# Layer 0's second product: one 512-column product for h's high part, and a bank emptied in two operations

## What is computed

```python
for i in range(e):                          # 8 experts, top 2 of them for each token
    h = jax.nn.silu(xf @ w1[i] + b1[i])     # 256 -> 1024
    y = h @ w2[i] + b2[i]                   # 1024 -> 256: the "second product"
    out = out + y * comb[:, i:i + 1]
```

## Time and profile before

| | |
|---|---|
| runs shown | 557.59, 560.01 and 751.81 us, median 560.01 |
| profiled execution | 557.76 us |
| its span, first to last instruction | 556.0 us |
| PE busy | 526.5 us, 95% |
| DVE busy | 329.5 us, 59% |
| POOL busy | 248.5 us, 45% |
| granted TensorE clock, mean | 0.995 of 2.4 GHz |

### The profile page before, as it was taken

How to read it: one execution, slowest core, us unless ns; L and a number is a source line. 1 busy time by engine, 2 the same in 40 slices (tenths; PEclk the granted TensorE clock), 3 DMA queues, 4 the chain that set the end, 5 groups by cost and what they waited for, 6 DMA issues and landing times.

```text
span 556.0 us, 15295 instructions
## 1 busy us (share of the span) xinstructions
PE 526.5 (95%) x3516; PEld 467.9 (84%) x3517; DVE 329.5 (59%) x770; ACT 339.9 (61%) x657; POOL 248.5 (45%) x278
## 2 busy tenths in 40 slices
PE   7999979999999999999999999799999999999995
PEld 3887638889999899999878876499999999999894
DVE  5647873555533555555575478745766666767542
ACT  5786625666655666666647856255677676767450
POOL 5659022343644355554354270224545364545432
PEclk9999999999999999999999999899999999999999
DMA  7645745876432454224550428463374656321211
GB/s 256 199 135 151 257 132 164 267 177 164 113 77 39 147 111 96 36 44 124 163 170 7 152 79 284 148 214 93 64 201 111 176 129 161 82 38 29 40 24 20
DMA packets 49037, 70.54 MB, mean 127 GB/s; under 512 B 9182, under 2 KB 40560, under 8 KB 49008
## 3 DMA queue, kind: packets, MB, share of 16 engines
q1 hardware_dynamic: 35216, 56.41, 32.3%
q0 software_dynamic: 10464, 13.58, 13.6%
q10 hardware_dynamic: 3328, 0.20, 0.4%
HBM read 57.55 MB, written 13.47 MB: 128 GB/s over the span
## 4 chain that ended last, share of the span: by engine, by line
PE 75%; DMA 6%; issue 5%; DVE 5%; ACT 3%; DVEq 3%; ACTq 1%; POOL 1%; POOLq 0%; SPq 0%
PE banks L1351 15%; PE banks L1353 15%; PE banks L1352 15%; PE banks L1576 5%; PE banks L1413 5%; PE banks L1501 4%; PE banks L1359 3%; PE banks L1477 3%; DMA expert_io<-xn_dram,gcol 2%; PE banks L1541 2%; PE banks L1631 2%; DMA mid_dram<-region_b,scol 1%; DVEq L1229 1%; PE banks L1424 1%; DMA xres<-in_x_dram 1%
## 5 line engine op out<-in xcount | busy, mean ns | idle before, releaser
L1351 PE MATMUL banks<-w_hi,xT_hi 128*128 x336 | 119.3, 355 | 4.3 <-DVE xT_lo L1220 2.6
L1353 PE MATMUL banks<-w_hi,xT_lo 128*128 x336 | 114.9, 342 | 0.0
L1352 PE MATMUL banks<-w_lo,xT_hi 128*128 x336 | 114.2, 340 | 0.0
L1351 PE MATMUL banks<-w_hi,hT_hi 128*128 x364 | 107.9, 296 | 3.7 <-DVE hT_lo L1298 2.7
L1353 PE MATMUL banks<-w_hi,hT_lo 128*128 x364 | 102.8, 283 | 0.0
L1352 PE MATMUL banks<-w_lo,hT_hi 128*128 x364 | 102.8, 282 | 0.0
L842 ACT COPY banks<-seed_rows 128x672 f32 (+1 forms) x84 | 69.0, 822 | 25.8 <-DVE h_sb L1315 10.3
L652 POOL DMA_INDIRECT mid_dram<-region_b,scol x26 | 49.6, 1909 | 77.3 <-DMA mid_dram<-region_b,scol 28.7
L625 POOL TENSOR_TENSOR w_lo<-raw,w_hi 128x1024 fp32r<-128x1024 f32 (+2 forms) x24 | 58.8, 2467 | 46.3 <-ACT w_hi L697 39.3
L652 POOL DMA_INDIRECT out_dram<-region_b,scol x26 | 46.1, 1772 | 72.2 <-DMA expert_io<-xn_dram,gcol 22.0
L1351 PEld LDWEIGHTS banks<-w_hi,hT_hi 128*128 128x128 f32 x364 | 69.3, 190 | 6.9 <-issue 6.0
(11 more groups left out here) (211 smaller groups left out, 872.0 us busy)
## 6 DMA issues: line engine op xcount, KB each, us to landing
raw<-in_L_ffn_w_dram SPq DMA_DIRECT2D x32, 512.0 KB, 3.8
raw<-in_L_ffn_W_dram SPq DMA_DIRECT2D x16, 672.0 KB, 3.9
seed_rows<-in_L_ffn_b_dram SPq DMA_DIRECT2D x8, 672.0 KB
seed_rows<-in_L_ffn_b_dram SPq DMA_DIRECT2D x8, 512.0 KB
xn_dram<-raw SPq DMA_DIRECT2D x6, 512.0 KB, 3.1
raw<-in_L_ffn_W_dram SPq DMA_DIRECT2D x8, 384.0 KB, 3.4
raw<-in_L_ffn_W_dram SPq DMA_DIRECT2D x8, 256.0 KB
wqkv<-in_L_conv_W_qkv_dram SPq DMA_DIRECT2D x2, 768.0 KB, 5.6
```

The source lines that it names most:

```text
L1351: pe.matmul(out, hi, w_high, start=first, stop=False, skip_group_check=onto)
L1352: pe.matmul(out, hi, w_low, start=False, stop=False, skip_group_check=onto)
L1353: return pe.matmul(out, lo, w_high, start=False, stop=last, skip_group_check=onto)
```

## The change

In layer 0 alone (layer 1 keeps its code):

1. `w_hi` and `w_lo` become two views of one tile `w_parts`, so that one operand can take the high and the low weights of the same rows, 256 columns each.
2. `second_product` first makes 8 matmuls of 512 columns: hT_hi[k] times (high | low), into all of bank 6. They wait for `hT_hi`, not for `hT_lo`. Then come 8 matmuls of 256 columns, hT_lo[k] times high, added to the bank's first half, and these wait for `hT_lo`.
3. DVE empties the bank in two operations of 128x256: the second half times the gate is added onto `gated_bias`, a new semaphore `e_low` says so, and then the old operation runs with that as its addend.

```diff
-        w_hi = sb("w_hi", [P, SLOTS, SLOT_WORDS], F32R)
-        w_lo = sb("w_lo", [P, SLOTS, SLOT_WORDS], F32R)
+        w_parts = sb("w_parts", [P, 2, SLOTS, SLOT_WORDS], F32R)
+        w_hi, w_lo = w_parts[:, 0, :, :], w_parts[:, 1, :, :]
...
                         dve.wait_ge(s.e_mm, b)
+                        if L == 0:
+                            nc.vector.scalar_tensor_tensor(out=gated_bias[:, :], in0=bank[6][:, C:2 * C],
+                                                           scalar=col(gate_tab, b - 1), in1=gated_bias[:, :],
+                                                           op0=ALU.mult, op1=ALU.add).then_inc(s.e_low, 1)
+                            dve.wait_ge(s.e_low, b)
...
+                    if L == 0:
+                        both = w_parts[:, :, e % SLOTS, KC * f.wide:KC * f.wide + f.kt * C].rearrange("p v (k n) -> p v k n", k=f.kt)
+                        for k in range(f.full):
+                            for j in range(2):
+                                if k == f.tiles[j].start:
+                                    pe.wait_ge(s.hT_hi, 2 * b + 1 + j)
+                            pe.matmul(bank[6][:, :], hT_hi[:, k, :], both[:, :, k, :], start=(k == 0), stop=(k == f.full - 1))
+                        for k in range(f.full):
+                            for j in range(2):
+                                if k == f.tiles[j].start:
+                                    pe.wait_ge(s.hT_lo, 2 * b + 1 + j)
+                            mm = pe.matmul(bank[6][:, 0:C], hT_lo[:, k, :], high[:, k, :], start=False, stop=(k == f.kt - 1),
+                                           skip_group_check=True)
```

More of the change, by code:

```diff
@@ L141, in __init__ @@
             self.gated = sem(f"gated_{L}")
+            self.e_low = sem(f"e_low_{L}")
         self.e_sb = sem(f"e_sb_{L}")
@@ L1583, in second_product @@
                         pe.wait_ge(s.e_sb, b)
[L1584 to L1589, removed]
+                    if L == 0:
[11 more added lines that the diff above has]
+                                           skip_group_check=True)
+                    else:
+                        for k in range(f.full):
+                            for j in range(2):
+                                if k == f.tiles[j].start:
+                                    pe.wait_ge(s.hT_lo, 2 * b + 1 + j)
+                            mm = product(bank[6][:, 0:C], hT_hi[:, k, :], hT_lo[:, k, :], high[:, k, :], low[:, k, :],
+                                         k == 0, k == f.kt - 1)
                     if f.tail:
```

## The result

The changed kernel takes **565.18 us** (median of 4 runs, 565.10 to 567.37), against 559.78 us for the kernel before in the same comparison: a ratio of **1.0126, 95% interval [1.0084, 1.0169]**. A second comparison, on another chip, gives 1.0158 [1.0084, 1.0231] with 564.33 us. The forecast was 558.0 us in a range to 561.4: it had a small gain, and there is a loss of 1.3 to 1.6%. It also took 2%, 11 us, as the least that a measurement can tell; the intervals are narrower than that, 0.2 to 0.7% to either side.

The account below looks back on a forecast made before the run. PE's own queue, 95% busy, was taken to bound layer 0's block loop except at late gathers. Terms +0.47, -2.3, +1.34 and -0.3 gave -0.79 us, from 558.8 to 558.0 us; range 554.9 to 561.4.

Parts of the forecast that it names:

- first blocks: Start of layer 0's loop: the gather PE waits for at 111.51 us moves with block 0's `e_sb`, +0.47 us.
- the layer's end: End of layer 0: PE loses two `hT_lo` waits, and `last_rows` start at about 276.8 instead of 277.11 us, -0.3 us.
- The merged product: Layer 0's second product: 16 matmuls instead of 24 save 0.10 us a block; 23 products in the sum, -2.3 us.
- Rival B: Second product: the merge saves nothing, as a two-piece operand pays 12.5 ns twice; 559.4 or 560.4 us; 0.13 together with D.
- D: Second product: PE loads the stationary part twice or loses time on register instructions; looks like Rival B, 0.13 together.
- The later `e_sb`: DVE's second emptying in layer 0 makes `e_sb` 0.57 us later, leaving 4.58 us to hide a gather instead of 5.25.
- The late ones: Layer 0 gathers behind 141.88 and 192.66 us, without margin: 0.67 us more each, +1.34 us.
- Rival A: Layer 0's late gathers do not move with `e_sb`, so a later start costs nothing: 554.9 or 555.9 us; chance 0.17.
- rival C: POOL's serial queue bounds more steps, 0.67 us a late gather; 560.7 us with six late, 561.4 with seven; chance 0.15.
- part 1: Layer 0's merged second product: each merge saves 0.0125 us, eight 0.10 us a block, 28 blocks 2.8 us.

Follow-up runs that it names:

- after_again: The changed kernel, unaltered, measured once more beside other versions on one chip: 564.33 us, ratio 1.0158 to the kernel before.
- pool_held: The changed kernel with POOL's fourth layer 1 weight piece held between the layers until the first `less_mean` is done: 563.76 us, ratio 1.0094.
- more_busy: The changed kernel with 13 instead of 5 PE filler matmuls between the layers, to fill PE's idle time: 565.17 us, ratio 1.0117.
- tile_only: The kernel before with `w_hi` and `w_lo` as views of one tile and nothing else: 560.8 us, ratio 1.0057.
- high_first: The kernel before with the 16 high-part products of layer 0 ordered first, no merge, no second emptying: 558.96 us, ratio 1.0028.
- empty_once: The changed kernel without the new DVE emptying; the product with the low weights is left in the bank: 559.6 us, ratio 1.0056.
- held_ahead: The changed kernel with POOL's gathers issued one scatter earlier and its fourth weight piece held until `less_mean` is done: 556.89 us, ratio 0.9961.
- tile_only_ahead: The kernel before with gathers issued one scatter earlier and `w_hi` and `w_lo` as views of one tile: 557.74 us, ratio 0.999.
- before_ahead: The kernel before with each POOL gather issued one scatter earlier and nothing else: 555.3 us, ratio 0.9959.
- after: The changed kernel itself in its first comparison with the kernel before: 565.18 us, ratio 1.0126; its profiled execution took 567.37 us.

## Why the prediction was wrong, point by point

The steps that failed are three: the sum's "first blocks" and "the layer's end" were sized too small, and the one tile was priced at nothing without a reason. The clock, which has no term, made the first two larger.

- **The merged product**: right in its mechanism, 0.08 us a block against 0.10, some 0.5 us too much over the layer. Rival B's nothing, or 0.02 us a block, did not come, and neither did D's slower matmuls.
- **The later `e_sb`**: right, 0.50 against 0.57 us, and what it does to a gather is right to the hundredth: one issued at 204.85 us is read at 209.42, 4.57 us later; forecast 4.58. The late ones cost 0.73 and 0.70 us more, forecast 0.67. Rival A is out. Of rival C this much is so: three gathers were late in the first profile, at 111, 141 and 196 us, the forecast's own three, but in after_again and pool_held PE also waited for the one before them (0.48 us at 104.21, 0.28 us at 104.40). C's price of 0.67 us a gather is not what made the loss.
- **"First blocks, +0.47"**: too small. From block 0 to block 6 it was +2.1 us. This term moved the gather but kept its 4.89 us. It took 6.57 us, 5.94 in after_again, 7.58 in pool_held and 7.75 in more_busy, whose layer 0 is the same, and 7.00 in tile_only; the step was 8.99, 7.65, 9.92 and 9.89 us in the four profiles of the changed kernel with the old gather order, against 7.97, and block 0 to block 6 cost +2.1, -0.2, +4.0 and +4.5 us (the last with a low clock at its start). The duration of a transfer that runs beside weight loads is no constant of the kernel; one row of it was taken for one. How much of its growth the later `e_sb` brings is open: tile_only and high_first, whose `e_sb` is not later, took 0.8 and 0.6 us more than the one profile of the kernel before. And a gap there cost clock: in all three with a step over 8.9 us, the step behind it took 8.35 to 8.45 us.
- **No term for the loop's last three steps**: +0.6 us. empty_once shows that they are the second emptying's. By which wait it reaches PE is not shown, since the profile has none over 0.1 us there.
- **"The layer's end, -0.3"**: wrong, +3.4 us to the next block loop. The first part of it gained nothing: counted from block 27, the one-hot table is 1.1 us late instead of 0.57, PE's two waits for `hT_lo` are replaced by two of the same length, and `last_rows` start 0.06 us later. And the working stopped at `last_rows`. It did not follow DVE's later table on to what else starts behind it, POOL's pieces, which now meet `less_mean`; that took 1.0 us. pool_held takes back all that was lost between the layers. The rest, about 2.4 us here and 1.1 in after_again, is a remainder and is put down to the low clock that both profiles have there.
- **Layer 1**: the largest error of reasoning. The forecast has no term for it because its code does not change, and part 1 priced the one tile at nothing without a sentence. It costs 2.3 to 3.2 us against before in every profile that has it, and tile_only measures 0.57% for it.
- **The clock** has no term in the sum at all. The kernel before keeps PE at 95% and nearly always at 2.4 GHz, and every new gap puts that at risk.

The sum again, in the profile's terms: start +0.7 (a low clock that is not shown to be the change's), loop +2.6, between the layers +3.4, layer 1 and end +2.7, together 9.5. In after_again, whose 563.85 us are closer to the median: +0.6, 0.0, +2.1, +3.2, together 6.0. So 3.5 us, 0.6% of the time, depend on which execution is profiled, and the tile's share is the steadiest.

With gathers ahead and POOL's piece held, the changed kernel is 0.4% faster than before (held_ahead, 0.9961). Beside the tile alone in the same batch (tile_only_ahead, 0.999) it is 0.85 us faster by the medians, and the intervals overlap; in the profiles it goes from block 0 to block 27 in 1.2 us less, which is about the merge's own gain, 24 times 0.08 us, less the 0.6 us of the last three steps. It does not beat the plain kernel with gathers ahead (before_ahead, 0.9959, from another batch), and the tile's price of about 2.2 us is enough to eat that gain. Both are faster than the two kernels of this case, and before_ahead needs only POOL's loop rewritten.

## What to carry to other kernels

- A tile's layout is part of every instruction that addresses it through a register. Before merging two tiles into one for the sake of one product, look at the queue instructions ahead of all their readers and writers, in all stages, at how long each takes as well as how many there are, and whether those queues have a lead.
- Where a kernel keeps its busiest engine at 95%, a saving or a delay early in it moves everything behind: follow the moved start to the next place where another engine works at the same time, and ask what collides there. Give the forecast a term for each such place, and a range on the late side wider than on the early one.
- If a wait ends with a transfer that shares its engines with others, take its price as a range from many executions, and try first to issue it earlier: here that alone is worth 0.4%, as much as the merge could have brought by itself (28 times 0.08 us).

## What the runs showed of the hardware that was not expected

- **A DVE operation with two inputs in SBUF does not end while a POOL operation that started before it runs.** `less_mean`, 128x4, took 1.37 us when it started 0.52 us into a 1.88 us operation of POOL, 0.33 when it started 1.56 us into it, and 0.16 with POOL idle. Other DVE operations are not held: L1336, with one input in PSUM, took its usual 0.48 us at 276.09 us, inside a POOL operation that ran from 275.22 to 277.65. The Trainium skill, page "SBUF — State Buffer", section "SBUF: two separate sides", says that a port pair of SBUF is locked for a whole instruction and that the other engine "fully blocks"; it names DVE operations with two SBUF inputs, against a POOL operation that reads SBUF, which these do. The rows agree: the held operation ended behind POOL's, by 0.01 to 0.03 us for `less_mean` and by 0.41 for L1032. The forecast should have weighed this page, and L1032 in its own trace, wherever it moved DVE against POOL.
- **A register-offset view of a merged tile makes a queue instruction longer**: 0.15 us instead of 0.06 on DVE ahead of a weight piece, and 0.046 instead of 0.032 on PE (an ISA in place of a REGISTER_ALU). No row before showed it.
- **The gather near 106 us took 5.94 to 7.75 us** in four executions of the same layer 0 (after, after_again, pool_held, more_busy), and 4.89 in the one of the kernel before.
- **A gap of 1.8 us in PE's work was followed by the 1.2 GHz level in three of six profiles.** Whether a given gap costs clock is not decided by the gap alone.
